# A fused attention and expert kernel: a new order of the first attention batch on all engines

## The chip, the cores and the metric

The kernel runs on one core of one Trainium2 chip. The metric is the device time of one execution in microseconds (us). TensorE is PE in the profile, VectorE DVE, ScalarE ACT, GpSimd POOL and SyncE SP. SP issues nearly all of the DMAs.

## The reference, cut to what matters

x is (2, 512, 1024), the context (2, 1024, 1024). Both x (after a layer norm) and the context are rounded to 8-bit integers, multiplied, and added to x. A second layer norm follows, then a gate that picks two of eight experts per token, and their matmuls.

```python
q1 = fake_quant(layernorm(x), s1, z1); q2 = fake_quant(ctx, s2, z2)   # (clip(round(v / s + z), 0, 255) - z) * s
x = x + tanh(g_xattn) * matmul(q1, q2)
y = layernorm(x)
top = top_k(y @ W_gate + b_gate, 2)
x = x + tanh(g_ffn) * mean over top of relu(y @ W_e + b_e)
```

## The kernel before, in words

Rows are handled in tiles of 128. There are eight x tiles (0 to 3 are batch 0, 4 to 7 batch 1) and sixteen context tiles (0 to 7 are batch 0). Every tile is 128 by 1024. There are three stages: the attention with the second layer norm and the gate (to about 90 us in the profile), the selection of experts (to about 109 us), and 20 expert slots, each 48 matmuls and 8 transposes.

The order of the work is written out by hand, one list for each engine, and every engine works its list strictly in order. Counting semaphores join the lists. All lines below are those of the profile.

A context tile k goes through these steps: SP loads it into one of eight slots of `stage` (`load_ctx`, L298; tile 8+k waits until tile k has been quantised), ACT or DVE writes it as 8-bit integers (`quantise_ctx`, L525 and L790, into one of four buffers `u8c`, so it waits for the centring of tile k-4), and POOL or DVE subtracts 128 and writes bf16 (`centre_ctx`, L424 and L795, tile `q2`). PE then adds its columns up (`column_sum`, L1057) and multiplies x tiles with it (`attend`, L1065).

An x tile i goes through these: SP loads it (`load_x`, L301), DVE takes mean and variance (`x_stats`, L744 and L746), ACT takes the root (`std`, L531), DVE makes scale and shift of two tiles at once with seven small operations (`scales`, L759 to L766), ACT or DVE writes 8-bit integers (`quantise_x`, L569 and L776), POOL or DVE centres them (`centre_q1`, L438 and L784), PE transposes (`transpose_q1`, L1050), ACT copies the result from PSUM (`keep_q1T`, L536), PE multiplies with the eight context tiles of the batch (`attend`), and then adds a correction that needs the batch's column sums (`fold`, L1072). DVE adds the product to x (`x_new`, L808), takes the second layer norm's statistics (`stats(1, ...)`), scales (L759 to L769), and DVE or ACT writes y (`normalise`, L802 and L549). PE transposes y (`transpose_y`, L1097), ACT copies it (`keep_yT`, L556), and PE makes the gate's product (`gate`, L1124: f32 matmuls with 8 columns each).

The column sums of a batch are copied by ACT (`keep_colsum_hi`, L541) when the eighth context tile has been added, and DVE then writes what the bf16 copy lost (`keep_colsum_lo`, L738). `fold` waits for that. `split_d` (L716 to L723) is a chain of small DVE operations that `fold` needs too. In `attend_after(i)` PE waits for an earlier `x_new`, since two PSUM slabs take turns, and for the tile's `keep_q1T`.

The expert weights of expert 0 are loaded into the same `stage` slots (`load_w0`, L305) and split by ACT (`split_hi0`, L561) and DVE (`split_lo`, L880).

Of the kernel before, what the change touches and what calls it, by code (L numbers as in the profile page):

```python
# [5 lines left out]
def flamingo_gated_moe(nc, x, ctx_kv, small, W_gate, W_e, b_e, out):  # L6
# [15 lines left out]
    KT = D // P  # L22
# [11 lines left out]
    NCH = 4  # L34
# [12 lines left out]
    with ctx:  # L47
# [186 lines left out]

        ACT_CTX = (0, 1, 2, 3, 4, 5, 8, 9, 10, 11, 12, 13, 14, 15)
        DVE_CTX = (6, 7)
        POOL_CEN = (0, 1, 2, 3, 5, 7, 8, 9, 10, 11, 12, 13, 14, 15)
        DVE_CEN = (4, 6)
        ACT_X, DVE_X = (0, 1, 2, 4, 5, 6, 7), (3,)
        POOL_Q1, DVE_Q1 = (0, 1, 2, 6), (3, 4, 5, 7)  # L240
        ACT_Y, DVE_Y = (1, 2, 6, 7), (0, 3, 4, 5)

        def wait_quantised_ctx(eng, k):
# [50 lines left out]
        def _(sp):  # L294
            def load_ctx(k):
                if k >= CB:
                    wait_quantised_ctx(sp, k - CB)
                sp.dma_start(stage[:, k % CB, :], ctx_t[k]).then_inc(s_ctx[k % CB], 16)  # L298

            def load_x(i):  # L300
                sp.dma_start(xt[:, i, :], x_t[i]).then_inc(s_x[i], 16)  # L301

            def load_w0(c):
                wait_quantised_ctx(sp, KT + 2 * c + 1)
                sp.dma_start(stage[:, CK * c:CK * (c + 1), :], w_t[:, 0, CK * c:CK * (c + 1), :]).then_inc(s_w[c], 16)  # L305
# [14 lines left out]

            for i in (0, 1):
                load_x(i)
            for k in (0, 1):
                load_ctx(k)
            load_x(2)
            load_ctx(2)
            load_x(3)
            for k in range(3, KT):
                load_ctx(k)
            for j in range(TPB):  # L330
                load_x(TPB + j)
                load_ctx(KT + j)
            sp.dma_start(wg[:, :, :], W_gate.rearrange("(k p) e -> p k e", p=P)).then_inc(s_wg, 16)
            for k in range(KT + TPB, 2 * KT):
                load_ctx(k)
            load_w0(0)
            load_w0(1)
            store_y(0)
            store_y(1)
            load_w0(2)  # L340
            load_w0(3)
            store_x_new(0)
            store_x_new(1)
            store_y(2)
# [46 lines left out]
        def _(pool):  # L391
# [49 lines left out]
            centre_ctx(1)  # L441
            centre_q1(0)
            centre_ctx(2)
            centre_q1(1)
            centre_ctx(3)
            centre_ctx(5)
            centre_ctx(7)
            centre_ctx(8)
            centre_q1(2)
            for k in range(KT + 1, 2 * KT):  # L450
                centre_ctx(k)
            pool.wait_ge(s_att, TPB)
            pool.iota(iota_pe[:, :, :], [[1, P], [0, E]], base=0, channel_multiplier=0,
                      allow_small_or_imprecise_dtypes=True).then_inc(s_iota, 1)
# [6 lines left out]
            add_rowsum(0)  # L461
            add_rowsum(1)
            centre_q1(6)
            add_rowsum(2)
            add_rowsum(3)

# [50 lines left out]
        def _(act):  # L517
            act.dma_start(par[:, :], small.partition_broadcast(P)).then_inc(s_par, 16)

            def quantise_ctx(k):  # L520

                act.wait_ge(s_ctx[k % CB], 16 * (k // CB + 1))
                if k >= 4:
                    wait_centred_ctx(act, k - 4)
                act.activation(u8c[:, k % 4, :], stage[:, k % CB, :], ACT.Identity, scale=dv(INV2),  # L525
                               bias=par[:, 3:4]).then_inc(s_uc, 1)

            def std(which, i, n, count):
# [65 lines left out]
            act.activation(drv[:, TX:TF + 1], par[:, 4:6], ACT.Tanh).then_inc(s_tanh, 1)  # L594
            act.wait_ge(s_const, 1)
            act.activation(lnv[:, 0, T1, 0:1], eps[:, :], ACT.Sqrt)
            std(0, 0, 2, 1)
            quantise_ctx(0)
            quantise_ctx(1)
            quantise_x(0)  # L600
            quantise_ctx(2)
            quantise_x(1)
            std(0, 2, 2, 2)
            quantise_ctx(3)
            keep_q1T(0)
            quantise_ctx(4)
            keep_q1T(1)
            quantise_ctx(5)
            quantise_x(2)
            quantise_ctx(8)  # L610
            keep_q1T(2)
            keep_colsum_hi(0)
            quantise_ctx(9)
            std(0, 4, 2, 3)
            quantise_ctx(10)
            quantise_x(4)
            quantise_ctx(11)
            keep_q1T(3)
            quantise_ctx(12)
            quantise_x(5)  # L620
            quantise_ctx(13)
            std(1, 0, 2, 1)
            quantise_ctx(14)
            normalise(1)
            quantise_ctx(15)
            keep_yT(0)
            keep_q1T(4)
            keep_q1T(5)
            std(1, 2, 2, 2)
            keep_yT(1)  # L630
            keep_colsum_hi(1)
            std(0, 6, 2, 4)
            normalise(2)
            sum_q1(4)
            quantise_x(6)
            quantise_x(7)
            split_hi0(0)
            keep_yT(2)
            keep_q1T(6)
            std(1, 4, 1, 3)  # L640
            sum_q1(5)
            keep_yT(3)
# [53 lines left out]
        def _(dve):  # L696
# [192 lines left out]
            scales(0, 0, 2, 1)  # L889
            x_stats(2)  # L890
            derive()
            x_stats(3)
            scales(0, 2, 2, 2)
            quantise_x(3)
            centre_q1(3)
            centre_ctx(4)
            quantise_ctx(6)
            centre_ctx(6)
            quantise_ctx(7)
            split_d()  # L900
            x_stats(4)
            x_stats(5)
            keep_colsum_lo(0)
            x_new(0)
            scales(0, 4, 2, 3)
            x_new(1)
            stats(1, 0, 0)
            centre_q1(4)
            stats(1, 1, 1)
            x_stats(6)  # L910
            x_new(2)
            scales(1, 0, 2, 1)
            normalise(0)
            x_new(3)
            read_rowsums()
            centre_q1(5)
            stats(1, 2, 0)
            stats(1, 3, 2)
            x_stats(7)
            scales(1, 2, 2, 2)  # L920
            keep_colsum_lo(1)
            scales(0, 6, 2, 4)
            normalise(3)
            x_new(4)
            centre_q1(7)
            stats(1, 4, 3)
            split_lo(0, 1, slice(0, CW))
            x_new(5)
            scales(1, 4, 1, 3)
            normalise(4)  # L930
            stats(1, 5, 4)
# [104 lines left out]
        def _(pe):  # L1036
# [120 lines left out]
                    wait_centred_ctx(pe, k)  # L1157
                    column_sum(k)

            column_sums(0, 2)  # L1160
            transpose_q1(0)
            column_sums(2, 3)
            transpose_q1(1)
            pe.wait_ge(s_qe, 1)
            for k in range(3):
                attend(0, k)
            for k in range(3, KT):
                column_sums(k, k + 1)
                attend(0, k)
                if k == KT - 2:  # L1170
                    transpose_q1(2)
            pe.wait_ge(s_qe, 2)
            attend_half(1, 0)
            attend_half(1, 1)
            pe.wait_ge(s_dr, 1)
            fold(0)
            fold(1)
            transpose_q1(3)
            for i in (2, 3):
                attend_after(i)  # L1180
# [28 lines left out]
            gate(2)  # L1209
            transpose_q1(7)  # L1210
            attend_half(6, 1)
# [86 lines left out]
```

## Time and profile before

| | us |
|---|---|
| median of 3 runs | 359.78 (358.92 to 360.76) |
| the profiled execution | 359.12, its span 357.4 |
| PE busy | 323.5 (91% of the span) |
| DVE busy | 226.3 (63%) |
| ACT busy | 139.9 (39%) |
| POOL busy | 113.0 (32%) |
| mean granted TensorE clock | 0.964 |

The page's busy times are averages over three stages with different limits. The times in the rows further down are microseconds from the start of the span. "Busy" of PE counts matmuls with modelled ends, so two neighbours overlap in the records, and the distance between starts tells the pace.

### The profile page before, as it was taken

The numbers are of one execution on the slowest core, as the hardware profiler recorded it, in microseconds if no ns is written. First come the engines' busy times: TensorE is split into PE (matmuls) and PEld (weight loads), VectorE is DVE, ScalarE is ACT, GpSimd is POOL, SyncE is SP. The second block draws the span as 40 slices with busy tenths as digits, with TensorE's granted clock in tenths as the row PEclk, the third lists the DMA queues.
The fourth block names the chain that finished last, engine by engine and source line by source line (L and its number), as shares of the span: only waits on it lengthen the run. The fifth ranks groups of instructions, "written<-read, shape, count | busy, mean of one in ns | idle before, by whom it ended". The sixth has DMA issues, their size and how long they took to land.

```text
span 357.4 us, 6929 instructions
## 1 busy us (share of the span) xinstructions
PE 323.5 (91%) x1695; PEld 251.0 (70%) x1704; DVE 226.3 (63%) x345; ACT 139.9 (39%) x124; POOL 113.0 (32%) x135
## 2 busy tenths in 40 slices
PE   0598899999599999999999999999999999999960
PEld 0134366589547888888888888888888888888840
DVE  2898999977889653799668326832349334934220
ACT  3774878789103701656172017201154015401100
POOL 3553464000024023415335335123332333233310
PEclk9999999998579999999999999999999999999995
DMA  6999568475327986799989955975439953455233
GB/s 224 413 409 385 220 253 347 166 261 230 159 85 300 410 285 135 192 383 318 417 251 326 358 125 131 395 237 117 88 103 358 330 109 86 100 116 118 29 88 59
DMA packets 23004, 81.46 MB, mean 228 GB/s; under 512 B 3152, under 2 KB 3152, under 8 KB 22992
## 3 DMA queue, kind: packets, MB, share of 16 engines
q1 hardware_dynamic: 16656, 58.76, 42.9%
q0 software_dynamic: 6192, 22.55, 26.6%
q8 instruction: 6, 0.10, 0.1%
q14 instruction: 6, 0.05, 0.0%
q10 hardware_dynamic: 144, 0.01, 0.0%
HBM read 62.43 MB, written 18.87 MB: 228 GB/s over the span
## 4 chain that ended last, share of the span: by engine, by line
PE 80%; DVE 12%; issue 2%; DMA 2%; POOL 1%; ACT 0%; POOLq 0%; DVEq 0%; ACTq 0%
PE ps L1262 61%; PE ps_y L1238 5%; PE ps L1065 4%; DVE st L744 4%; PE ps_q L1124 2%; PE ps_s L1124 2%; PE ps L1042 2%; PE ps_y L1097 2%; DMA par<-in_small_dram 2%; DVE xt L808 1%; PE ps L1150 1%; PE ps L1072 1%; DVE u8c L790 1%; DVE lnv L760 1%; DVE mv L746 1%
## 5 line engine op out<-in xcount | busy, mean ns | idle before, releaser
L1262 PE MATMUL ps<-w_hi,yT_hi 128*128 x320 | 126.5, 395 | 0.5 <-DVE yT_lo L994 0.5
L1262 PE MATMUL ps<-w_hi,yT_lo 128*128 x320 | 124.8, 390 | 0.0
L1262 PE MATMUL ps<-w_lo,yT_hi 128*128 x320 | 124.5, 389 | 0.0
L880 DVE TENSOR_TENSOR w_lo<-stage,w_hi 128x2048 f32 (+1 forms) x32 | 72.0, 2287 | 13.2 <-ACT w_hi L679 11.8
L679 ACT ACTIVATE w_hi<-stage 128x2048 f32 x28 | 52.5, 1912 | 59.1 <-PE ps L1262 47.2
L504 POOL DMA_INDIRECT out_dram<-res,sidx x20 | 32.5, 1627 | 133.7 <-DVE res L1028 121.1
L1025 DVE TENSOR_TENSOR res<-ps,bias 128x512 f32<-128x512 f32 x40 | 27.6, 689 | 65.5 <-issue 34.1
L1262 PEld LDWEIGHTS ps<-w_hi,yT_hi 128*128 128x128 f32 x320 | 60.1, 188 | 12.7 <-issue 0.9
L1262 PEld LDWEIGHTS ps<-w_hi,yT_lo 128*128 128x128 f32 x320 | 60.1, 188 | 12.8
L1262 PEld LDWEIGHTS ps<-w_lo,yT_hi 128*128 128x128 f32 x320 | 60.2, 188 | 11.8
L666 ACT ACTIVATE yT_hi<-ps_y 128x1024 fp32r<-128x1024 f32 x21 | 21.4, 1020 | 114.5 <-PE ps_y L1238 114.5
L994 DVE TENSOR_TENSOR yT_lo<-ps_y,yT_hi 128x1024 fp32r<-128x1024 f32 x21 | 25.7, 1223 | 19.2 <-ACT yT_hi L666 12.3
L1065 PE MATMUL ps<-q,q1T 128*128 128x512 bf16 x123 | 31.2, 396 | 2.4 <-ACT q1T L536 1.8
L473 POOL DMA_INDIRECT y_rows<-y_scratch,gidx x22 | 24.4, 1109 | 17.7 <-POOL gidx L470 17.7
L470 POOL COPY gidx<-idx 128x1 uint32 x22 | 24.2, 1098 | 6.5 <-PE ps_y L1238 5.1
L1065 PEld LDWEIGHTS ps<-q,q1T 128*128 128x128 bf16 x128 | 12.6, 102 | 17.0 <-issue 3.5
L424 POOL TENSOR_SCALAR q<-u8c 128x1024 bf16<-128x1024 uint8 x14 | 15.5, 1108 | 26.8 <-ACT u8c L525 26.1
L1238 PE MATMUL ps_y<-ident_f,y_rows 128*128 128x128 f32 x168 | 21.8, 273 | 0.0
L1028 DVE TENSOR_SCALAR res<-res,weight 128x512 f32<-128x512 f32 x40 | 19.5, 486 | 3.7 <-DVE res L1025 1.4
L1238 PEld LDWEIGHTS ps_y<-ident_f,y_rows 128*128 128x128 f32 x168 | 19.5, 140 | 3.0 <-DMA y_rows<-y_scratch,idx 0.4
L744 DVE BATCH_NORM_STATS2 st<-xt 128x6 f32<-128x512 f32 x32 | 20.5, 683 | 0.4
L1057 PE MATMUL ps_y<-q,ones_b 128*128 128x512 bf16 x15 | 6.8, 542 | 12.9 <-POOL q L424 12.8
(163 smaller groups left out, 264.7 us busy)
## 6 DMA issues: line engine op xcount, KB each, us to landing
stage<-in_L_ffn_W_e_dram SPq DMA_DIRECT2D x32, 1024.0 KB, 7.3
stage<-in_ctx_dram SPq DMA_DIRECT2D x16, 512.0 KB, 11.6
xt<-in_x_dram SPq DMA_DIRECT2D x8, 512.0 KB, 11.4
y_scratch<-y SPq DMA_DIRECT2D x8, 512.0 KB, 3.9
out_dram<-xt SPq DMA_DIRECT2D x8, 512.0 KB, 3.0
bias<-in_L_ffn_b_e_dram SPq DMA_DIRECT2D x8, 512.0 KB, 4.2
y_rows<-y_scratch,gidx POOLq DMA_INDIRECT x22
out_dram<-res,sidx POOLq DMA_INDIRECT x20, 6.4
```

Of the source, the lines that this page charges most:

```text
L470: pool.tensor_copy(gidx[:, q:q + 1], idx[:, bass.ds(col, 1)]).then_inc(s_pool, 1)
L473: pool.indirect_dma_start(out=y_rows[q][:, :], out_offset=None, in_=y_dram[:, :], in_offset=bass.IndirectOffsetOnAxis(ap=gidx[:, q:q + 1], ...
L504: pool.indirect_dma_start(out=out_rows[:, :], out_offset=bass.IndirectOffsetOnAxis(ap=sidx[:, q:q + 1], axis=0), in_=res[q][:, :], in_offs ...
L666: act.activation(yT_hi[q][:, :, :], ps_y[:, :, :], ACT.Copy).then_inc(s_eh, 1)
L679: act.activation(w_hi[:, bass.ds((nxt & 1) * WSZ + c * CW, CW)], stage[:, CK * c:CK * (c + 1), :].rearrange("p k h -> p (k h)"), ACT.Copy) ...
L744: last = dve.bn_stats(st[:, which, h, :], xt[:, i, h * 512:(h + 1) * 512])
L880: dve.tensor_tensor(w_lo[:, dst], stage[:, CK * c:CK * (c + 1), :].rearrange("p k h -> p (k h)"), w_hi[:, dst].bitcast(f32), ALU.subtract) ...
L994: dve.tensor_tensor(yT_lo[q][:, :, :], ps_y[:, :, :], yT_hi[q][:, :, :].bitcast(f32), ALU.subtract).then_inc(s_el, 1)
L1025: dve.tensor_tensor(res[q][:, half], ps[q][:, half], bias[:, bass.ds((woff >> 3) + h * 512, 512)], ALU.add).then_inc(s_free, 1)
L1065: pe.matmul(ps[slab(i)][:, h * 512:(h + 1) * 512], q1T[:, i, k % KT, :], q2[:, k, h * 512:(h + 1) * 512], start=(k % KT == 0), stop=False)
L1238: last = pe.transpose(ps_y[:, k, :], y_rows[q][:, k * P:(k + 1) * P], ident_f[:, :])
L1262: last = pe.matmul(ps[q][:, h * 512:(h + 1) * 512], lhs[q][:, k, :], w[:, bass.ds(woff + k * D + h * 512, 512)], start=(k == 0 and lhs is ...
```

## The change

The lists of all five engines are changed in the attention stage. On SP, context tile 2 is loaded ahead of x tile 2, x tile 3 after context tile 7, and x tiles 6 and 7 after all context tiles. The four loads of expert 0's weights stand together ahead of the first stores of y. Context tiles 6 and 7 are centred on DVE (before: 4 and 6), tile 4 and 5 on POOL. Tiles 4, 5 and 7 of x are centred on POOL and no longer on DVE. ACT quantises context tiles ahead of the roots and x tiles. DVE does the quantising and centring of context tiles 6 and 7 before the statistics of x tile 3, and does the statistics of x tiles 6 and 7 after `keep_colsum_lo(1)`. PE adds up three context tiles first, transposes x tile 2 after the two folds, adds up the second batch's eight context tiles ahead of x tile 5's transpose, and transposes each y tile later in the list. Nothing that is computed changes.

```diff
-        POOL_CEN = (0, 1, 2, 3, 5, 7, 8, 9, 10, 11, 12, 13, 14, 15)
-        DVE_CEN = (4, 6)
+        POOL_CEN = (0, 1, 2, 3, 4, 5, 8, 9, 10, 11, 12, 13, 14, 15)
+        DVE_CEN = (6, 7)
-        POOL_Q1, DVE_Q1 = (0, 1, 2, 6), (3, 4, 5, 7)
+        POOL_Q1, DVE_Q1 = (0, 1, 2, 4, 5, 6, 7), (3,)
...
 # SP
-            for k in (0, 1):
+            for k in (0, 1, 2):
                 load_ctx(k)
             load_x(2)
-            load_ctx(2)
-            load_x(3)
             for k in range(3, KT):
                 load_ctx(k)
+            load_x(3)
+            load_ctx(KT)
+            load_ctx(KT + 1)
+            load_x(4)
+            load_ctx(KT + 2)
+            load_x(5)
...
-            load_w0(0)
-            load_w0(1)
+            load_x(6)
+            load_x(7)
+            for c in range(NCH):
+                load_w0(c)
             store_y(0)
             store_y(1)
-            load_w0(2)
-            load_w0(3)
...
 # ScalarE
+            act.wait_ge(s_inv, 1)
+            quantise_ctx(0)
             std(0, 0, 2, 1)
-            quantise_ctx(0)
             quantise_ctx(1)
+            quantise_ctx(2)
             quantise_x(0)
-            quantise_ctx(2)
             quantise_x(1)
+            quantise_ctx(3)
+            quantise_ctx(4)
+            keep_q1T(0)
+            quantise_ctx(5)
+            keep_q1T(1)
+            quantise_ctx(8)
+            keep_colsum_hi(0)
             std(0, 2, 2, 2)
...
+            quantise_ctx(15)
+            quantise_x(4)
             quantise_x(5)
...
             keep_q1T(4)
             keep_q1T(5)
-            std(1, 2, 2, 2)
+            std(1, 0, 2, 1)
+            keep_colsum_hi(1)
+            normalise(1)
+            keep_yT(0)
+            sum_q1(4)
+            std(0, 6, 2, 4)
             keep_yT(1)
...
             quantise_x(6)
             quantise_x(7)
+            std(1, 2, 2, 2)
             split_hi0(0)
+            keep_q1T(6)
+            normalise(2)
             keep_yT(2)
-            keep_q1T(6)
...
 # VectorE
             derive()
+            split_d()
+            quantise_ctx(6)
+            quantise_ctx(7)
+            centre_ctx(6)
+            centre_ctx(7)
             x_stats(3)
             scales(0, 2, 2, 2)
+            keep_colsum_lo(0)
             quantise_x(3)
             centre_q1(3)
...
+            x_new(0)
             x_stats(4)
+            x_new(1)
             x_stats(5)
+            x_new(2)
             scales(0, 4, 2, 3)
             stats(1, 0, 0)
+            x_new(3)
             stats(1, 1, 1)
+            read_rowsums()
             scales(1, 0, 2, 1)
             normalise(0)
+            keep_colsum_lo(1)
+            x_stats(6)
+            x_stats(7)
             stats(1, 2, 0)
+            scales(0, 6, 2, 4)
+            x_new(4)
             stats(1, 3, 2)
             scales(1, 2, 2, 2)
             normalise(3)
+            x_new(5)
...
 # TensorE
-            column_sums(0, 2)
+            column_sums(0, 3)
             transpose_q1(0)
-            column_sums(2, 3)
             transpose_q1(1)
+            column_sums(3, 4)
...
             fold(0)
             fold(1)
+            transpose_q1(2)
             transpose_q1(3)
...
             column_sums(KT, KT + 4)
             transpose_q1(4)
-            transpose_y(0)
-            column_sums(KT + 4, KT + 6)
+            column_sums(KT + 4, 2 * KT)
             pe.wait_ge(s_rs, 1)
             transpose_q1(5)
-            transpose_y(1)
-            column_sums(KT + 6, 2 * KT)
             attend_after(4)
             attend_half(4, 0)
-            gate(0)
+            transpose_y(0)
             attend_half(4, 1)
             fold(4)
-            transpose_y(2)
+            transpose_y(1)
+            gate(0)
...
             fold(5)
-            transpose_y(3)
+            transpose_y(2)
             attend_after(6)
             attend_half(6, 0)
+            transpose_y(3)
             gate(2)
```

## Rows read from the trace of the kernel before

**Rows 1.** Busy time by stretch: start:end, length, five engines, PEclk, DMA share, GB/s

```profile
34.50:56.50 22.00, 20.37 (x146) 11.51 (x150) 20.82 (x44) 16.69 (x19) 10.30 (x11) 1.00 0.70 269
56.50:90.30 33.80, 33.64 (x237) 26.18 (x240) 27.61 (x66) 29.28 (x33) 3.67 (x3) 0.94 0.63 241
90.30:109.00 18.70, 14.31 (x111) 8.82 (x111) 16.44 (x50) 1.42 (x2) 3.38 (x5) 0.66 0.32 113
```

**Rows 2.** The chain that ended last: start, length, engine, tile, line

```profile
28.37 0.38 PE ps_y L1057
...
33.21 1.30 DVE xt L808
...
55.21 1.23 DVE cs L738
...
70.86 0.54 PE ps L1072 x2
```

**Rows 3.** Timeline of PE: start, length, line, operation, output, shape, count, idle time before

```profile
19.20 2.74 PE L1065 MATMUL ps<-q,q1T 128*128 128x512 bf16 x6 [0.79 <-ACT q1T L536]
...
24.86 0.59 PE L1057 MATMUL ps_y<-q,ones_b 128*128 128x512 bf16 x2
...
34.55 3.63 PE L1065 MATMUL ps<-q,q1T 128*128 128x512 bf16 x16 [0.40 <-DVE xt L808]
...
46.72 1.09 PE L1097 MATMUL ps_y<-ident_f,y 128*128 128x128 f32 x8
...
51.06 1.89 PE L1065 MATMUL ps<-q,q1T 128*128 128x512 bf16 x7
52.78 1.85 PE L1124 MATMUL ps_s<-wg,yT 128*128 128x8 f32 x16
```

**Rows 4.** Timeline of ACT

```profile
29.28 1.02 ACT L541 ACTIVATE cs<-ps_y 128x1024 bf16<-128x1024 f32 x1
30.18 1.24 ACT L525 ACTIVATE u8c<-stage,par,drv 128x1024 uint8<-128x1024 f32 x1
31.31 0.29 ACT L531 ACTIVATE lnv<-mv,eps 128x2 f32<-128x2 f32 x1
...
60.31 1.89 ACT L561 ACTIVATE w_hi<-stage 128x2048 fp32r<-128x2048 f32 x1
```

**Rows 5.** Timeline of DVE

```profile
10.45 0.17 DVE L759 RECIPROCAL lnv<-lnv 128x2 f32<-128x2 f32 x1 [0.43 <-ACT lnv L531]
...
11.30 0.23 DVE L764 TENSOR_SCALAR lnv<-lnv,drv 128x2 f32<-128x2 f32 x1
...
11.76 0.90 DVE L766 TENSOR_SCALAR lnv<-lnv,par 128x2 f32<-128x2 f32 x1
...
22.96 1.53 DVE L790 TENSOR_SCALAR u8c<-stage,drv,par 128x1024 uint8<-128x1024 f32 x1
...
50.24 1.29 DVE L744 BATCH_NORM_STATS2 st<-xt 128x6 f32<-128x512 f32 x2
51.56 0.21 DVE L746 BATCH_NORM_AGGREGATE mv<-st 128x2 f32<-128x12 f32 x1
...
58.03 0.81 DVE L802 TENSOR_SCALAR y<-xt,lnv 128x1024 f32<-128x1024 f32 x1
```

**Rows 6.** Timeline of POOL

```profile
11.57 2.17 POOL L424 TENSOR_SCALAR q<-u8c 128x1024 bf16<-128x1024 uint8 x2 [7.67 <-ACT u8c L525]
...
22.40 1.55 POOL L424 TENSOR_SCALAR q<-u8c 128x1024 bf16<-128x1024 uint8 x1 [3.01 <-ACT u8c L525]
```

**Rows 7.** Timeline of SP: the issues of context tile 0 and of x tile 4

```profile
1.77 0.42 SPq L298 DMA_DIRECT2D stage<-in_ctx_dram  x1
...
7.30 0.46 SPq L301 DMA_DIRECT2D xt<-in_x_dram  x1
```

**Rows 8.** The same two among the DMA issues: count, KB, us from issue to landing

```profile
stage<-in_ctx_dram SPq DMA_DIRECT2D x1, 512.0 KB, 7.3
...
xt<-in_x_dram SPq DMA_DIRECT2D x1, 512.0 KB, 14.6
```

More of the change, by code:

```diff
@@ L322, in _ @@
                 load_x(i)
-            for k in (0, 1):
+            for k in (0, 1, 2):
                 load_ctx(k)
             load_x(2)
-            load_ctx(2)
-            load_x(3)
             for k in range(3, KT):
                 load_ctx(k)
-            for j in range(TPB):
-                load_x(TPB + j)
-                load_ctx(KT + j)
+            load_x(3)
[4 more added lines that the diff above has]
+            load_x(5)
+            load_ctx(KT + 3)
+            load_ctx(KT + 4)
             sp.dma_start(wg[:, :, :], W_gate.rearrange("(k p) e -> p k e", p=P)).then_inc(s_wg, 16)
-            for k in range(KT + TPB, 2 * KT):
+            for k in range(KT + 5, 2 * KT):
                 load_ctx(k)
-            load_w0(0)
-            load_w0(1)
+            load_x(6)
+            load_x(7)
+            for c in range(NCH):
+                load_w0(c)
             store_y(0)
             store_y(1)
-            load_w0(2)
-            load_w0(3)
             store_x_new(0)
@@ L441, in _ @@
             centre_ctx(1)
+            centre_ctx(2)
             centre_q1(0)
-            centre_ctx(2)
             centre_q1(1)
             centre_ctx(3)
+            centre_ctx(4)
             centre_ctx(5)
-            centre_ctx(7)
             centre_ctx(8)
+            centre_ctx(9)
+            centre_ctx(10)
             centre_q1(2)
-            for k in range(KT + 1, 2 * KT):
+            for k in range(KT + 3, 2 * KT):
                 centre_ctx(k)
+            centre_q1(4)
+            centre_q1(5)
             pool.wait_ge(s_att, TPB)
@@ L463, in _ @@
             centre_q1(6)
+            centre_q1(7)
             add_rowsum(2)
@@ L596, in _ @@
             act.activation(lnv[:, 0, T1, 0:1], eps[:, :], ACT.Sqrt)
+            act.wait_ge(s_inv, 1)
+            quantise_ctx(0)
             std(0, 0, 2, 1)
-            quantise_ctx(0)
             quantise_ctx(1)
+            quantise_ctx(2)
             quantise_x(0)
-            quantise_ctx(2)
             quantise_x(1)
-            std(0, 2, 2, 2)
[L604 to L608, printed above, removed]
+            quantise_ctx(3)
[5 more added lines that the diff above has]
+            keep_colsum_hi(0)
+            std(0, 2, 2, 2)
+            quantise_ctx(9)
+            quantise_ctx(10)
             quantise_x(2)
-            quantise_ctx(8)
+            quantise_ctx(11)
             keep_q1T(2)
[L612 to L617, printed above, removed]
             keep_q1T(3)
             quantise_ctx(12)
-            quantise_x(5)
[L621 to L626, printed above, removed]
+            quantise_ctx(13)
+            quantise_ctx(14)
+            std(0, 4, 2, 3)
+            quantise_ctx(15)
+            quantise_x(4)
+            quantise_x(5)
             keep_q1T(4)
             keep_q1T(5)
-            std(1, 2, 2, 2)
+            std(1, 0, 2, 1)
[4 more added lines that the diff above has]
+            std(0, 6, 2, 4)
             keep_yT(1)
[L631 to L634, printed above, removed]
             quantise_x(6)
             quantise_x(7)
+            std(1, 2, 2, 2)
             split_hi0(0)
+            keep_q1T(6)
+            normalise(2)
             keep_yT(2)
-            keep_q1T(6)
             std(1, 4, 1, 3)
@@ L891, in _ @@
             derive()
+            split_d()
[3 more added lines that the diff above has]
+            centre_ctx(7)
             x_stats(3)
             scales(0, 2, 2, 2)
+            keep_colsum_lo(0)
             quantise_x(3)
             centre_q1(3)
[L896 to L900, printed above, removed]
+            x_new(0)
             x_stats(4)
+            x_new(1)
             x_stats(5)
-            keep_colsum_lo(0)
-            x_new(0)
+            x_new(2)
             scales(0, 4, 2, 3)
-            x_new(1)
             stats(1, 0, 0)
-            centre_q1(4)
+            x_new(3)
             stats(1, 1, 1)
-            x_stats(6)
-            x_new(2)
+            read_rowsums()
             scales(1, 0, 2, 1)
             normalise(0)
-            x_new(3)
-            read_rowsums()
-            centre_q1(5)
+            keep_colsum_lo(1)
+            x_stats(6)
+            x_stats(7)
             stats(1, 2, 0)
+            scales(0, 6, 2, 4)
+            x_new(4)
             stats(1, 3, 2)
-            x_stats(7)
             scales(1, 2, 2, 2)
-            keep_colsum_lo(1)
-            scales(0, 6, 2, 4)
             normalise(3)
-            x_new(4)
-            centre_q1(7)
+            x_new(5)
             stats(1, 4, 3)
             split_lo(0, 1, slice(0, CW))
-            x_new(5)
             scales(1, 4, 1, 3)
@@ L1158, in column_sums @@
                     column_sum(k)
-            column_sums(0, 2)
+            column_sums(0, 3)
             transpose_q1(0)
-            column_sums(2, 3)
             transpose_q1(1)
+            column_sums(3, 4)
             pe.wait_ge(s_qe, 1)
-            for k in range(3):
+            for k in range(4):
                 attend(0, k)
-            for k in range(3, KT):
+            for k in range(4, KT):
                 column_sums(k, k + 1)
                 attend(0, k)
-                if k == KT - 2:
-                    transpose_q1(2)
             pe.wait_ge(s_qe, 2)
```

## The prediction

> **What bounds the kernel now.** I read the busy times by stretch first [rows 1]. From 34.50 us to 90.30 PE is the bound: it is busy 20.37 of 22.00 us and then 33.64 of 33.80. From 90.30 to 109.00 it waits on the selection, and behind that the slots follow at a fixed pace. No work outside the attention stage changes, so the question is only how far the end of that stage moves. I then read the chain of waits for where PE depended on others [rows 2]: the last column sum of batch 0 at 28.37, `x_new(0)` at 33.21 (it frees PE for x tile 2), `keep_colsum_lo(1)` at 55.21 (`fold(4)` waits for it), and `fold(6)` at 70.86 + 0.54 = 71.40. From there on both lists have the same PE order, and PE is dense. So I work out when `fold(6)` ends after the change; the difference to 71.40 is the difference of the whole. It splits at the start of `attend(2)`, 34.55 before [rows 3].
>
> **Prices.** PE: an x tile against eight context tiles is 3.6 us with the fold 4.1, half of it 1.72 (51.06 to 52.78), a y transpose 0.93 (the 1.09 without its overlap), a gate 1.71 (1.85 without it) [rows 3]; two matmuls of 512 columns start to start take 0.84 at 19.20 (six in 2.53) and 0.44 from 24.86 on. These are the two levels of the clock, 1.2 and 2.4 GHz, though the granted clock is given as 1.00 for both. ACT: a copy 0.90 (29.28 to 30.18), a quantisation 1.13 in a row and 1.24 to its end, a root 0.29, a weight split 1.89 [rows 4]. DVE: statistics of a tile 1.54 (50.24 to 51.56 + 0.21), seven small operations of a `scales` 1.6 or, in the second norm, five in 1.0 (0.2 each, 10.45 to 11.76), y 0.81, `keep_colsum_lo` 1.23, `x_new` 1.30 [rows 2, 5]. POOL: a centring 1.04 [rows 6]. An idle engine starts about 0.06 after its releaser, DVE 0.4 after a root starts.
>
> **Where DVE and POOL collide.** DVE's L764 takes 0.23, and L766, a like operation, takes 0.90 with POOL's centring (11.57 to 12.61) beside it [rows 5, 6]: it ends at 12.66, when POOL's first one does. The quantisation at 22.96 took 1.53, not 0.81, beside POOL's of 22.40, itself 1.55. So such an operation waits for the other engine's to end. The Trainium skill says so too (SBUF — State Buffer, "Who interferes with whom"): whoever issues first holds the shared pair of ports for the whole instruction, and the other one blocks. This case's trace agrees (0.90 against 0.23). By a reading without that rule the sum below would be 1.4 us less. The rule speaks against this change, which puts POOL's first centrings on top of the first `scales`.
>
> **Part 1: up to the start of attend(2).** Loads: context tile 0 lands at 1.77 + 7.3 = 9.07, x tile 4, ten transfers later, at 21.90, so 1.28 a tile [rows 7, 8]. In the new order context tile 2 lands at 11.6, x tile 2 at 12.9, context tiles 3 to 7 from 14.2 to 19.3 (1.28 earlier each), x tile 3 at 20.6 (6.4 later), context tile 8 at 21.9. x tiles 6 and 7 land by 37; their use is after 50. The bytes are the same.
> - ACT quantises context tile 0 at 9.15 to 10.38 and is then behind with the root: DVE begins `scales` at 10.68 (before 10.45). POOL now centres at 10.46 to 11.5, 11.8 to 12.8 and 13.0 to 14.0. Three operations of `scales` are caught, one by each, so it ends at 14.05 and not at 12.66. x tile 0 is quantised at 14.1 to 15.3, x tile 1 to 16.5, POOL centres them by 16.5 and 17.6, and PE transposes from 16.55. ACT then does two context tiles ahead of `keep_q1T(0)`, which ends at 19.65. `attend(0)` starts at 19.7 (19.20 before). The gain in loading is not in it.
> - DVE ends `split_d` at 20.35 (the same 3.6 with POOL beside it as before, now ahead of the context tiles), quantises tiles 6 and 7 to 22.6 and centres them to 23.95.
> - PE from 19.7: 11 units of 0.86 or 0.44 us (one context tile's sum or product) to the last column sum. Before, the pace rose at 24.3, 5.1 us behind the dense start at 19.20. PE is dense from 16.55 now, so I take 21.7; at once would give the last sum at 24.7, as late as before 26.3. Taken: T = 25.5, where it was 28.75.
> - Behind T: ACT's copy to T + 1.05, the root, `scales` for x tiles 2 and 3 from T + 1.4 (new there; the root stood ahead of this before), its last operation caught by POOL, to T + 3.55, `keep_colsum_lo(0)` to T + 4.8, then the folds. `quantise_x(3)` to T + 5.65, `centre_q1(3)` behind POOL's `centre_q1(2)` to T + 7.1, `x_new(0)` to T + 8.45. `attend(2)` starts at T + 8.5 = 34.0. Before, from 28.75 to 34.55 it took 5.8. So 3.25 us gained at T shrink to 0.55.
>
> **Part 2: from attend(2) at 34.0 to fold(6).** PE's work is the same, 71.40 - 34.55 = 36.85 less 1.6 idle (22.00 - 20.37) = 35.25. I look for PE's new waits.
> - `x_new(1)` is done at 36.8, so `attend(3)` follows at once; with fold to 42.1. Row sums, four context sums, the transpose of x tile 4 (POOL has it at 44.2, after `scales(0, 4)` to 41.8), four sums to 47.0, the transpose of x tile 5 to 47.55, the first half of `attend(4)` to 49.2. No wait so far.
> - `transpose_y(0)` wants y(0). Its root now stands on ACT behind `keep_q1T(5)`, which waits for PE's 47.55: copy 47.6, root 48.5, `scales` to 49.9, y(0) at 50.75. **PE waits 1.6.** Then y transpose 51.75, half 53.45, `fold(4)` 54.0 (`keep_colsum_lo(1)`, 51.95, no longer holds it), y transpose 54.95, gate 56.65, half 58.4, gate 60.1.
> - `transpose_q1(6)`: DVE goes on behind `keep_colsum_lo(1)` with x tiles 6 and 7 and `stats(1, 2)`, 3 x 1.54, to 56.55, `scales(0, 6)` to 58.2, ACT 59.5, POOL 60.6. **PE waits 0.55**, transposes to 61.15, half 62.85, `fold(5)` 63.4.
> - `transpose_y(2)`: `x_new(4)` to 59.5, `stats(1, 3)` to 61.05, root, then on ACT `split_hi0(0)` 61.45 to 63.35, a copy to 64.2, y(2) to 65.4. **PE waits 2.05.** y(3), by DVE at 63.5, is in time, so from 65.45: transpose, half, transpose, gate, q transpose, half, fold: 0.93 + 1.72 + 0.93 + 1.71 + 0.5 + 1.7 + 0.55 = 8.05, `fold(6)` ends at 73.5.
> - Check: 34.0 + 35.25 + 4.2 = 73.45. So +2.1 against 71.40: -0.55 in part 1, +4.2 of new waits, -1.6 of old ones.
>
> **Edits at nothing.** The fourth weight load now stands ahead of the y stores on SP and waits for context tile 15's quantisation, at about 40; y(0) is there at 50.75. Three centrings go from DVE to POOL, which is idle then (10.30 of 22.00 [rows 1]); DVE's relief is what takes `keep_colsum_lo(1)` off the path, and it is in the sum. If the y stores were late, `normalise(4)` would be; it has 7 us to spare.
>
> **The sum.** The profiled execution took 359.12, so 359.12 + 2.1 = 361.2. The median of the runs is 0.66 above it, by which it would be 361.9. I take the middle, 361.5.
>
> **Bounds.** T: -0.8 to +0.8 (pace). Collisions: none caught in the first `scales` takes 0.7 off T (DVE's context tiles then bound), none in the second takes 0.65; one more adds 0.9. The wait for y(0) is 1.3 to 1.9. That for y(2) is at least 0.5, if ACT were free when the scale is ready, at most 2.5. Not all go one way: 0 to +4.3, so 358.9 to 363.9 between the two bases.
>
> **The rivals.**
> - *Faster: the new waits do not appear.* If the roots and y tiles come in time, PE's 35.25 us stand dense behind 33.2 to 34.0: `fold(6)` at 68.5 to 69.3, 2.1 to 2.9 less, 356.2 to 357.3. For it: PE loses nothing through `keep_colsum_lo(1)`, and DVE is relieved. Against: y(0)'s root stands behind a copy that waits for PE, whatever DVE does. Chance 0.14, with halfway cases.
> - *No change: the collisions miss.* They hang on a tenth or two of a microsecond. Without them `attend(2)` starts 0.7 to 1.4 earlier, and the sum is +0.7 to +1.4: 360.2 to 360.8. Chance 0.38, with the case that y(2) is less late.
> - *Slower still: the clock falls in the waits.* From 90.30 to 109.00, with PE busy 14.31 of 18.70, the granted clock is 0.66 [rows 1]. If a wait of 1.6 or 2.05 beside gates of 8 columns did that, some 5 us (19.2 to 24.3) would run at 0.84 for 0.44: +2.4, 363.9. Against: waits of 1.0 us did not do it. Chance 0.06.
> - The forecast has the rest, 0.42.
>
> **How the numbers follow.** A measurement can tell 0.5% from nothing, 1.8 us here, so 361.6 is the edge, and the forecast lies on it. I count the forecast's case as slower (what of it falls below the edge, the no-change case's upper end makes up): slower 0.42 + 0.06 = 0.48, same 0.38, faster 0.14. The range leaves out the dense rival's core and the upper bound of all waits together: 358.0 to 364.0.
>
> **What would show it.** In the profile after: `attend(0)` starts near 19.7, the last column sum of batch 0 near 25.5, `attend(2)` near 34.0. PE's list of waits has new ones on ps_y for y (L1097), 1 to 2 us each, released by `normalise`. `fold(6)` ends near 73.5. I am wrong if `attend(2)` starts below 32, or if PE meets y(0) and y(2) without waiting, or if stretches behind 90 us change in length.

## The result, and the profile after

The changed kernel took 364.64 us (median of 4, 364.27 to 364.97) against 359.57: a ratio of 1.0123, 95% interval 1.0098 to 1.0148 (the quotient of the two medians, 1.0141, lies within it). Ratios compare fast executions alone: one that lies over 1.5% above the fastest of its kernel is left out, as the one of 367.07 in run 5. The change is slower, as forecast, but by 5 us and not by 2, and outside the range. The profiled execution took 364.40 with a span of 362.7, against 359.12 and 357.4: 5.28 us to explain.

The busy times of the same three stretches as [rows 1], with the same columns:

```profile
34.50:56.50 22.00, 19.84 (x126) 9.28 (x126) 16.61 (x35) 14.40 (x15) 11.06 (x12) 0.92 0.62 247
56.50:90.30 33.80, 31.61 (x239) 23.97 (x238) 28.78 (x68) 26.99 (x33) 6.43 (x4) 1.00 0.60 224
90.30:109.00 18.70, 14.94 (x115) 11.55 (x115) 15.20 (x52) 4.35 (x5) 1.37 (x2) 0.54 0.34 129
```

PE is less busy in both of the first two, and the granted clock, 1.00 before, is 0.92 in the first. The timeline of PE answers to [rows 3]:

```profile
19.71 3.15 PE L1071 MATMUL ps<-q,q1T 128*128 128x512 bf16 x8
...
25.29 0.59 PE L1063 MATMUL ps_y<-q,ones_b 128*128 128x512 bf16 x2
...
30.83 1.02 PE L1078 MATMUL ps<-cs,d_rows 64*128 64x512 bf16 x4 [1.06 <-DVE cs L747]
...
33.88 0.62 PE L1056 MATMUL ps_s<-ident_b,q 128*128 128x128 bf16 x8 [1.37 <-DVE q L793]
35.20 5.31 PE L1071 MATMUL ps<-q,q1T 128*128 128x512 bf16 x16 [0.70 <-DVE xt L817]
...
40.98 3.63 PE L1071 MATMUL ps<-q,q1T 128*128 128x512 bf16 x16
...
53.59 1.09 PE L1103 MATMUL ps_y<-ident_f,y 128*128 128x128 f32 x8 [1.46 <-DVE y L811]
...
63.51 0.62 PE L1056 MATMUL ps_q<-ident_b,q 128*128 128x128 bf16 x8 [0.43 <-POOL q L441]
...
68.15 1.09 PE L1103 MATMUL ps_y<-ident_f,y 128*128 128x128 f32 x8 [1.76 <-ACT y L557]
...
75.65 0.60 PE L1078 MATMUL ps<-cs,d_rows 64*128 64x512 bf16 x2
```

The reader is to see four things. `attend(0)` starts at 19.71, and the last column sum starts at 25.29, 3.1 us earlier than before. `attend(2)` starts at 35.20, 0.65 later than before; the gain is gone by then. It takes 5.31 us where `attend(3)`, the same 16 matmuls, takes 3.63. Three waits stand behind it, 3.65 us together. `fold(6)` starts at 75.65 and ends at 76.26 by the chain, 4.86 behind 71.40 [rows 2].

The PE busy time and granted clock around `attend(2)` (stretch, length, PE busy, PEclk, DMA share, GB/s):

```profile
34.00:36.00 2.00, 1.30 (x12) 0.98 1.04 414
36.00:38.00 2.00, 2.00 (x7) 0.50 1.03 410
38.00:40.00 2.00, 2.00 (x8) 0.66 1.04 412
40.00:42.00 2.00, 2.00 (x10) 1.00 1.00 397
```

The clock fell to 0.50, its 1.2 GHz level, near 36, and came back before 40. Ahead of it PE had waited 1.06 + 1.37 + 0.70 = 3.13 of the 5.43 us from 29.77 to 35.20, and done only the four matmuls of two folds and two transposes. Before, it had waited 0.40 there [rows 3].

The waits of the kernel before are less than the 1.6 that its busy time leaves. Two lines of its PE:

```profile
39.74 3.40 PE L1065 MATMUL ps<-q,q1T 128*128 128x512 bf16 x15 [1.02 <-ACT q1T L536]
...
70.80 0.60 PE L1072 MATMUL ps<-cs,d_rows 64*128 64x512 bf16 x2
```

The trace has 15 of the 16 matmuls of `attend(3)`, and 7 of 8 in some halves; each missing record of 0.22 us counts as idle. So I take the distance instead. With the changed kernel's 40.98 - 40.45 = 0.53 for a fold, `attend(3)` could have started at 38.11 + 0.53 = 38.64. From there to `fold(6)` it is 70.80 - 38.64 = 32.16. In the changed kernel it is 75.65 - 40.98 = 34.67, of which 3.65 are waits and 31.02 work. The same work leaves 32.16 - 31.02 = 1.14 of old waits.

| where | us |
|---|---|
| start of attend(2), 35.20 - 34.55 | 0.65 |
| attend(2) at the lower clock, 5.25 - 3.56 to the start of its fold | 1.69 |
| waits behind it, 3.65 - 1.14 | 2.51 |
| rounding between there and fold(6) | 0.01 |
| behind fold(6): the last gates (95.24 - 89.51 for 90.11 - 84.65: 0.27) and the rest | 0.42 |
| sum | 5.28 |

### The profile page after: what moved, and what is told of

Read it like the earlier page. It is cut to its first block, busy times and chain, and to the rows that moved or that the text cites. A ratio compares the mean times of both kernels' runs of the same rounds, so it can differ in the third digit from the quotient of the medians.

```text
span 362.7 us, 6937 instructions
## 1 busy us (share of the span) xinstructions
PE 325.6 (90%) x1703; PEld 251.1 (69%) x1704; DVE 225.5 (62%) x342; ACT 140.9 (39%) x124; POOL 118.1 (33%) x138
## 4 chain that ended last, share of the span: by engine, by line
PE 80%; DVE 8%; DMA 3%; issue 3%; ACT 2%; POOL 1%; SPq 0%; POOLq 0%; DVEq 0%; ACTq 0%
PE ps L1266 60%; PE ps L1071 6%; PE ps_y L1242 5%; PE ps_q L1130 2%; DMA stage<-in_ctx_dram 2%; PE ps_y L1103 2%; PE ps_s L1130 1%; DVE st L753 1%; DMA y_rows<-y_scratch,idx 1%; PE ps L1156 1%; PE ps L1063 1%; PE ps_y L1063 1%; DVE xt L817 1%; DVE cs L747 1%; ACT u8c L533 1%
## 5 line engine op out<-in xcount | busy, mean ns | idle before, releaser
L1000 DVE TENSOR_TENSOR yT_lo<-ps_y,yT_hi 128x1024 fp32r<-128x1024 f32 x21 | 25.7, 1222 | 18.9 <-ACT yT_hi L675 12.2
L1071 PE MATMUL ps<-q,q1T 128*128 128x512 bf16 x128 | 33.0, 407 | 0.7 <-DVE xt L817 0.7
L481 POOL DMA_INDIRECT y_rows<-y_scratch,gidx x22 | 24.4, 1111 | 17.7 <-POOL gidx L478 17.7
L1242 PEld LDWEIGHTS ps_y<-ident_f,y_rows 128*128 128x128 f32 x168 | 19.5, 140 | 3.2 <-DMA y_rows<-y_scratch,idx 0.6
L1034 DVE TENSOR_SCALAR res<-res,weight 128x512 f32<-128x512 f32 x40 | 19.5, 486 | 3.6 <-DVE res L1031 0.6
```

The lines of the kernel that those rows point to most:

```text
L481: pool.indirect_dma_start(out=y_rows[q][:, :], out_offset=None, in_=y_dram[:, :], in_offset=bass.IndirectOffsetOnAxis(ap=gidx[:, q:q + 1], ...
L1000: dve.tensor_tensor(yT_lo[q][:, :, :], ps_y[:, :, :], yT_hi[q][:, :, :].bitcast(f32), ALU.subtract).then_inc(s_el, 1)
L1071: pe.matmul(ps[slab(i)][:, h * 512:(h + 1) * 512], q1T[:, i, k % KT, :], q2[:, k, h * 512:(h + 1) * 512], start=(k % KT == 0), stop=False)
L1242: last = pe.transpose(ps_y[:, k, :], y_rows[q][:, k * P:(k + 1) * P], ident_f[:, :])
```

## The experiments

Each ratio is against the kernel before, run beside it on the same chip. The kernels start from the changed one, unless it is said.

**1. Fillers ahead of attend(2).**

```diff
+            fill(4, ps_s[:, :])          # fill: n matmuls of 512 columns into an unused PSUM bank
             fold(0)
             fold(1)
             transpose_q1(2)
+            fill(5, ps_k[:, 0:512])
             transpose_q1(3)
+            fill(3, ps_k[:, 0:512])
```

> The changed kernel with 12 filler matmuls of 512 columns (into PSUM that nobody needs then) in the three gaps of PE ahead of attend(2): 4 before the folds, 5 and 3 behind the transposes of x tiles 2 and 3. Theory (clock): attend(2) took 5.31 us because PE had idled 3.1 us of the 5.4 before it and the granted clock fell to 0.50 behind that. Then it takes 3.6 again, starts no later than 35.3, and the whole is 1.7 us less than the changed kernel: about 362.9. Rival (something else slowed the matmuls, as the DMAs and GpSimd beside them): attend(2) keeps 5.3 and the time stays at 364.6.

Measured: 364.04 (362.57 to 365.82), ratio 1.0099 (1.0072 to 1.0125); the profiled execution took 362.78. Its PE (the line numbers are five higher here):

```profile
34.52 3.63 PE L1076 MATMUL ps<-q,q1T 128*128 128x512 bf16 x15
...
61.17 0.62 PE L1061 MATMUL ps_q<-ident_b,q 128*128 128x128 bf16 x8 [0.43 <-POOL q L441]
61.84 3.00 PE L1076 MATMUL ps<-q,q1T 128*128 128x512 bf16 x7
...
65.81 1.09 PE L1108 MATMUL ps_y<-ident_f,y 128*128 128x128 f32 x8
```

`attend(2)` takes 3.63 with DMAs and POOL beside it as in the changed kernel, so the mechanism is shown. The other traces bear it out. From the start of `attend(2)` to its fold it is 5.25 to 5.77 us in all five kernels with this order and no fillers (the changed one, both of run 4, those of runs 6 and 7), and 3.55 or 3.56 in the three with fillers there (runs 1 to 3).

But the clock now fell at 61.84 (half a tile in 3.00 and not 1.89 us), behind a gate and a short wait. That fall cost nothing by `fold(6)`: the wait of 1.76 for y(2) is gone at 65.81, since PE came later and y(2) was ready. From `attend(2)` to `fold(6)` it is 38.79 us against 40.45, and the profiled execution is 1.6 less than the changed kernel's, both near the 1.7 expected. The median gained little, and the ten times spread over 3 us where the changed kernel's four lay within 0.7. Their mean granted clocks go from 0.949 (at 365.82) to 0.963 (at 363.11).

**2. Fillers in every gap.** Six more ahead of `transpose_y(0)`, two ahead of `transpose_q1(6)`, seven ahead of `transpose_y(2)`.

> The changed kernel with filler matmuls of 512 columns in every gap of PE: the 12 ahead of attend(2), and 6 ahead of transpose_y(0), 2 ahead of transpose_q1(6), 7 ahead of transpose_y(2). Theory (new waits, and a clock that falls because of them, at one place or another from execution to execution): the granted clock stays at 1.00 up to the last gates, attend(2) takes 3.6 us, and what is left against the kernel before are the waits alone, 3.65 us less the 1.6 of old ones: fold(6) ends near 73.2, 2 us behind the kernel before (ratio 1.005 to 1.006), with less spread than the 12 fillers alone. Rival (the fillers delay PE, or the clock is not what they touch): ratio 1.010, as with the 12 alone.

Measured: median 364.56, ratio 1.009 (1.0053 to 1.0127). The nine times lie in two groups: 361.07, 361.09 and 361.50, and six from 364.30 to 365.68. By the medians (364.56 and 360.03) the quotient would be 1.0126. The profile is of the lower group (361.50):

```profile
19.60 2.31 PE L1076 MATMUL ps<-q,q1T 128*128 128x512 bf16 x8
...
24.34 0.59 PE L1068 MATMUL ps_y<-q,ones_b 128*128 128x512 bf16 x2
...
34.25 3.63 PE L1076 MATMUL ps<-q,q1T 128*128 128x512 bf16 x16
...
73.05 0.60 PE L1083 MATMUL ps<-cs,d_rows 64*128 64x512 bf16 x2
```

and its granted clock by stretch:

```profile
28.00:44.00 16.00, 15.43 (x108) 1.00 1.04 397
44.00:84.00 40.00, 39.69 (x276) 1.00 0.54 202
```

With the clock at 1.00 throughout, `fold(6)` starts at 73.05 and ends near 73.6, 2.2 behind the kernel before. That is the forecast's sum (73.5), but in part by luck. The last column sum starts at 24.34, 0.95 ahead of the changed kernel's 25.29, since PE's pace rose sooner in `attend(0)` (2.31 for its eight matmuls, there 3.15). The fillers stand behind that, so they are not the reason. From the last column sum to `attend(2)` it is 9.91 in both. With the changed kernel's own start, 35.20, the same 38.80 us would put `fold(6)` at 74.00, 3.2 behind the kernel before.

The median did not follow. The mean granted clock is on record for each execution: 0.964 or 0.965 in the lower group, 0.958 or 0.959 in the upper. So a fall of the clock goes with the 3 us between them, in spite of the fillers. Where it falls then is not known, as no trace of the upper group was kept.

**3. Fillers behind the gates too.** Three more behind each of gates 0 to 4, where PE has no gap.

> As the kernel with fillers in every gap, and 3 more fillers of 512 columns behind each of gates 0 to 4, where PE has no gap: 15 x 0.22 = 3.2 us of added work, about 3.0 on PE's path. Theory (the gates' 8-column matmuls are what lets the clock fall, and the executions of the kernel with filled gaps near 364.5 are those in which it fell behind a gate): no execution falls there, the times lie in one group, at 361.3 + 3.0 = 364.3, as low as the slow group before it although PE does 3 us more. Rival (the slow group has another cause, a DMA or GpSimd): two groups again, 364.3 and 367.6.

Measured: 366.24, six times within 0.9 us (366.14 to 367.04), ratio 1.0154 (1.0124 to 1.0185).

```profile
28.00:84.00 56.00, 54.89 (x372) 1.00 0.67 250
84.00:97.00 13.00, 13.00 (x80) 0.70 0.62 251
```

One group, as the theory had it, and the clock holds to 84. But it lies 1.9 above what was expected. Nine of the 15 fillers stand ahead of `fold(6)`, 1.9 us, so run 2's 73.05 would become 75.0; it starts at 74.73, and the stretch up to there is not the reason. The last gates run from 90.23 to 96.91, 6.68 us, against 5.46 before and 5.31 in run 2, and the transpose ahead of them is slow as well: the clock falls earlier against them. Why there is only one group is thus not wholly shown. The fillers may also just have moved the falls to the end.

**4. The waits for y(0) and y(2).** On ScalarE, alone and then both:

```diff
             keep_q1T(4)
+            std(1, 0, 2, 1)
             keep_q1T(5)
-            std(1, 0, 2, 1)
...
-            split_hi0(0)
             keep_q1T(6)
             normalise(2)
+            split_hi0(0)
```

> The changed kernel with the root for y tiles 0 and 1 (std(1, 0)) ahead of keep_q1T(5) on ScalarE, not behind it. Theory (the chain over DVE binds): the 1.46 us that PE waits for y(0) go, but x tile 6 and y(2) come only as much earlier as DVE starts keep_colsum_lo(1) earlier, 1.1 us, and PE's waits there grow by 0.3: 1.1 us less, 363.5. Rival (PE's waits add up): 1.46 less, 363.2, with the later waits as they were (0.43 and 1.76). Second rival (it moves on): nothing, the wait reappears at transpose_y(2), 364.6.

> As the run before (root for y(0) first), and also split_hi0(0) behind normalise(2) on ScalarE instead of ahead of keep_q1T(6). Theory: y(2) then comes 1.2 us behind its scale and PE's wait for it falls from 1.76 to about 0.4; together 2.5 us less than the changed kernel, 362.1. Rival (DVE's chain to the scale of y(2) is what binds, ScalarE's order is cover): no more than the run before, 363.5.

Measured: 364.53, ratio 1.0118 (1.0069 to 1.0167), and 365.33, ratio 1.0116 (1.0061 to 1.0170). No gain that can be told. PE in the first:

```profile
52.71 1.04 PE L1103 MATMUL ps_y<-ident_f,y 128*128 128x128 f32 x8
...
63.10 0.62 PE L1056 MATMUL ps_q<-ident_b,q 128*128 128x128 bf16 x8 [0.96 <-POOL q L441]
63.77 3.14 PE L1071 MATMUL ps<-q,q1T 128*128 128x512 bf16 x7
...
67.74 1.09 PE L1103 MATMUL ps_y<-ident_f,y 128*128 128x128 f32 x8
...
75.24 0.60 PE L1078 MATMUL ps<-cs,d_rows 64*128 64x512 bf16 x2
```

The wait for y(0) is gone, and that for x tile 6 has grown from 0.43 to 0.96. From the start of `attend(3)` to that of `fold(6)` it is 75.24 - 41.73 = 33.51, against 34.67 in the changed kernel: 1.16 less, as expected. It is that although the clock fell at 63.77 (granted 0.61 from 63.0 to 66.8) and took about 1.2: PE comes to y(2) so much later, at 67.74, that the wait of 1.76 is gone, and the fall costs nothing by `fold(6)`. What hid the gain lies outside. `attend(3)` started 0.75 later (41.73 for 40.98), 0.23 of it ahead of the last column sum and 0.52 in `attend(2)`, where the clock fell earlier; and PE waited 0.51 for a y tile's copy behind `fold(6)`.

In the second kernel `fold(6)` starts at 73.63, 2.0 earlier than in the changed one, 0.7 of it from an earlier last column sum. But the clock fell again, where no wait stood behind to take it up:

```profile
82.76 3.19 PE L1071 MATMUL ps<-q,q1T 128*128 128x512 bf16 x7 [0.20 <-issue]
```

The last gates took 6.69 us there for 5.73, and ended 2.4 later than the changed kernel's.

**5. x_new(0) first on VectorE.**

```diff
+            x_new(0)
             quantise_x(3)
             centre_q1(3)
-            x_new(0)
...
 # TensorE, in the loop over x tiles 2 and 3 (and no longer ahead of it)
                 attend_half(i, 0)
+                if i == 2:
+                    transpose_q1(3)
                 attend_half(i, 1)
```

> The changed kernel with x_new(0) ahead of quantise_x(3) and centre_q1(3) on DVE, and PE transposing x tile 3 between the two halves of attend(2) instead of ahead of it. Theory (the collisions of DVE with GpSimd and the queue behind the folds set the start of attend(2)): it starts at 33.6, when keep_q1T(2) is done, instead of 35.2; PE idles 2.2 instead of 3.1 us before it, so the clock may hold: 1.6 us less if it falls all the same (363.0), 3.2 less if it holds (361.4). Rival (x tile 3, now 1.3 us later, becomes the wait at attend(3)): no gain, 364.6.

Measured: 364.20 (361.46 to 367.07), ratio 1.0077 (1.0044 to 1.0109). `attend(2)` starts at 33.59, as expected, 8.42 behind the last column sum and not 9.91. The clock holds over it (1.00) without a filler, behind waits of 1.06 and 1.21, 2.27 us together for 3.13. In the profiled execution, 365.41, it fell later (stretch, length, PE busy, PEclk, DMA share, GB/s):

```profile
62.00:66.00 4.00, 3.95 (x17) 0.64 0.00 0
66.00:71.00 5.00, 4.59 (x19) 0.61 0.75 301
```

**6. GpSimd waits for VectorE.** One line, `pool.wait_ge(s_q1, 1)`, ahead of `centre_ctx(11)`.

> The changed kernel with GpSimd waiting for centre_q1(3) of VectorE before it centres context tile 11. Theory (collision): centre_q1(3) takes 0.7 instead of 1.41 us, x_new(0) and attend(2) start 0.7 earlier (34.5 for 35.2); the clock falls all the same; 0.3 to 1.0 less than the changed kernel, within what 3 rounds can tell. Rival (the length of that operation is its own): 1.41 as before.

Measured: 363.78, ratio 1.0089 (1.0053 to 1.0126). The operations on VectorE in the changed kernel, and then in this one (its line numbers are one higher):

```profile
28.34 0.16 DVE L774 SCALAR_TENSOR_TENSOR lnv<-mv,lnv 128x2 f32<-128x2 f32 x1
28.53 0.90 DVE L775 TENSOR_SCALAR lnv<-lnv,par 128x2 f32<-128x2 f32 x1
29.47 1.22 DVE L747 TENSOR_TENSOR cs<-ps_y,cs 32x1024 bf16<-32x1024 f32 x1
30.72 1.67 DVE L785 TENSOR_SCALAR u8x<-xt,lnv 128x1024 uint8<-128x1024 f32 x1
32.42 1.41 DVE L793 TENSOR_SCALAR q<-u8x 128x1024 bf16<-128x1024 uint8 x1
```

```profile
28.36 1.04 DVE L775 SCALAR_TENSOR_TENSOR lnv<-mv,lnv 128x2 f32<-128x2 f32 x1
29.44 1.11 DVE L776 TENSOR_SCALAR lnv<-lnv,par 128x2 f32<-128x2 f32 x1
...
31.84 1.66 DVE L786 TENSOR_SCALAR u8x<-xt,lnv 128x1024 uint8<-128x1024 f32 x1
33.53 0.69 DVE L794 TENSOR_SCALAR q<-u8x 128x1024 bf16<-128x1024 uint8 x1
```

The centring takes 0.69 and not 1.41: the collision is shown. But `attend(2)` started at 35.60, where 34.5 was expected: the same execution lost more elsewhere. POOL's centring began at 28.35, 0.01 ahead of the small operation at 28.36, which then took 1.04 and not 0.16. In the changed kernel POOL began at 28.34 too, and the operation slipped through. Nothing in the lists decides that. The 1.67 of `quantise_x(3)` stays (1.66): the edit does not touch the centring beside it.

**7. The load order of before, all else changed.**

> The changed kernel with the load order of the kernel before for the first batch (x tile 2 ahead of context tile 2, x tile 3 ahead of context tile 3), all other lists as changed. Theory (the earlier landing of the context tiles is not on the path: PE's first products wait for the quantised x tiles, and context tile 7 waits for VectorE): no change against the changed kernel, 364.6, attend(0) within 0.1 of 19.7. Rival (the loads do bound batch 0): 1.3 us more, 365.9.

Measured: 364.90, ratio 1.0115 (1.0074 to 1.0157), against 1.0123 for the changed kernel. The interval alone would hardly exclude the rival's 1.3 us; the trace does: `attend(0)` starts at 19.60 (19.71 in the changed kernel) and the last column sum at 25.00 (25.29). The earlier loads bring nothing.

**8. The repairs together.** As expected below; the second time without the swap on VectorE.

> The changed kernel with what the runs so far point to, together: root for y(0) ahead of keep_q1T(5), split_hi0(0) behind normalise(2), x_new(0) ahead of quantise_x(3), x tile 3 transposed between the halves of attend(2), scales(0, 4) ahead of x_new(2), and fillers ahead of the folds (4), of attend(2) (5) and of transpose_q1(6) (4). Theory (order behind the folds loses what the earlier context tiles gain): attend(2) starts near 33.3, no wait above 1 us behind it, fold(6) ends at 70.5 to 71.5 against 71.4 before: ratio 0.997 to 1.001. Rival (DVE's chain has no slack, each repair moves the wait): ratio 1.007 as with x_new first alone.

> The repaired kernel without its swap on VectorE, that is with x_new(2) ahead of scales(0, 4) as in the changed kernel. Theory (the swap made the waits of 1.5 us for x_new(2) and 0.7 us for the row sums): both go, a wait of 0.85 for q1 of x tile 4 comes; 1.3 us less than the repaired kernel, fold(6) at 71.9 to 72.0 where the clock holds, ratio 1.003 to 1.005. Rival: the ratio stays at 1.0085, as the clock's falls make up the most of it.

Measured: 363.94, ratio 1.0085 (1.0056 to 1.0114), and 361.81 (360.71 to 364.34), ratio 1.0037 (1.0011 to 1.0063). The swap was a mistake: it made PE wait 1.5 us for `x_new(2)` and 0.7 for the row sums. Without it PE waits 0.85, 0.30 and two gaps that fillers cover, and `fold(6)` starts at 71.17, 0.4 behind the kernel before (from `attend(2)` on 1.33 less than with the swap, as expected):

```profile
71.17 0.60 PE L1083 MATMUL ps<-cs,d_rows 64*128 64x512 bf16 x2
...
79.78 3.18 PE L1076 MATMUL ps<-q,q1T 128*128 128x512 bf16 x7 [0.22 <-issue]
```

In that execution (363.97) the clock fell at 79.78, in `attend(7)`. It is the changed order at its best here, and not better than the old one.

**9. One part alone, and from the kernel before.** GpSimd centres x tiles 4, 5 and 7 in the kernel before; then also:

```diff
             quantise_ctx(10)
+            keep_q1T(3)
             quantise_x(4)
             quantise_ctx(11)
-            keep_q1T(3)
```

> The kernel before with one part of the change alone: GpSimd centres x tiles 4, 5 and 7 instead of VectorE, each at its old place among the context tiles. Theory: VectorE is relieved of 3.4 us (1.16, 0.68 and 1.55), but PE is dense from 34.5 on and waited for it only 0.1 us at fold(4) and 1.0 at attend(3): 0 to 0.8 us less, ratio 0.998 to 1.000. Rival (GpSimd's extra operations hit VectorE's small ones): up to 0.8 more.

> The kernel before with GpSimd centring x tiles 4, 5 and 7, and keep_q1T(3) ahead of quantise_x(4) on ScalarE, which is idle there for 3.4 us, instead of behind quantise_ctx(11). Theory (from attend(2) on PE is the bound in that kernel, and its one wait of 1 us there is for this copy): the wait of 1.02 ahead of attend(3) goes and fold(6) ends 1 us earlier, near 70.4: ratio 0.996 to 0.998. Rival (the time reappears at fold(4) or in the clock): ratio 0.9995 to 1.002.

Measured: 360.17 beside 360.03, ratio 0.9995 (0.9969 to 1.0020), and 360.00 beside 360.65, ratio 0.9973 (0.9952 to 0.9995). The second is the only kernel here whose interval lies below 1, and that by 0.0005 only; among so many kernels it might be chance, but its trace shows the gain. Its PE:

```profile
34.59 3.63 PE L1067 MATMUL ps<-q,q1T 128*128 128x512 bf16 x16 [0.40 <-DVE xt L813]
...
38.91 3.40 PE L1067 MATMUL ps<-q,q1T 128*128 128x512 bf16 x15 [0.16 <-issue]
...
69.72 0.60 PE L1074 MATMUL ps<-cs,d_rows 64*128 64x512 bf16 x2
```

The wait of 1.02 ahead of `attend(3)` is down to 0.16, and `fold(6)` starts at 69.72 and not 70.80: 1.1 us. (Both waits have a missing record of 0.22 in them.)

## Why the prediction was wrong

- **Part 1, up to the last column sum: right.** `attend(0)` at 19.7 was 19.71. T, taken as 25.5, was 25.29 + 0.4 = 25.7. The three collisions in the first `scales` were there, and it ended at 14.1 (14.05 worked out). That loading is not on the path is shown by run 7. The upper bound of T was worked out too low: with the pace rising 5.1 behind 19.7, as before, the 11 units end at 27.0 and not at 26.3. In the traces of runs 1 to 8 the eight matmuls of `attend(0)` take from 2.02 to 3.50 us, and T goes from 24.4 to 25.95, so one trace says little on this term.
- **Part 1, from T to attend(2): 1.0 us too little.** 8.5 was worked out, 9.5 measured. I let VectorE's `quantise_x(3)` win against POOL. It lost, 1.67 and not 0.81; the 1.41 of `centre_q1(3)` was in the sum. The Trainium skill (SBUF — State Buffer, "Who interferes with whom") lets issue order decide. Run 6 agrees for the small operation, where 0.01 us did. For `quantise_x(3)` the records do not show it: VectorE's starts at 30.72 and GpSimd's centring at 30.79, and it is VectorE's that takes twice its time. The upper bound of "one more collision, 0.9" held this. With T it makes the start 35.20, not 34.0.
- **Part 2, "PE's work is the same", 35.25 us: the step that failed.** The lists have the same work, but it ran at two clocks. `attend(2)` was priced at 3.6, and took 5.25 to its fold, 1.7 more, because of the 3.13 us idle ahead of it. I had those gaps in my own numbers (folds at T + 4.8, the wait for `x_new(0)`) and never added them up. I looked at waits only as lost time, and put the fall of the clock as a rival with 0.06, at the waits for y, where in this kernel it did not occur. Its price, 2.4, was of the right order (1.7). Run 1 shows the cause: 12 fillers, and 3.63 us. The 35.25 was also 0.46 too low on its own, since 1.6 of old idle time was taken off and only 1.14 was there.
- **Part 2, the new waits: right.** 1.6, 0.55 and 2.05 were forecast, 1.46, 0.43 and 1.76 measured, each with the releaser named. Run 4 shows the y(0) chain as it was told, with its onward growth at x tile 6.
- **The sum.** Run 2's executions at the full clock take 361.07 to 361.50, where the forecast was 361.2 by the profiled base and 361.5 on record. That they meet is in part luck, since in the one that was traced T was 0.95 earlier than in the changed kernel. The changed kernel's own trace gives 5.28 - 1.69 = 3.6 without the fall of the clock, where 2.1 was summed. The missing 3.2 are the clock in `attend(2)` (1.7), the later start (1.2), the old waits (0.46) and what lies behind `fold(6)` (0.42), less 0.55 for new waits shorter than forecast.
- **The range** was too narrow above, since each term's upper end was priced alone. A fall of the clock belonged among the bounds, as did its coming together with one more collision. Either alone would have stayed inside 364.0.
- **Still open:** why the clock fell in some executions of a kernel and not in others, and what each such fall is worth. It is not the change's alone: of the 26 executions of the kernel before beside run 2, 25 lie from 359.11 to 362.65, those up to 360.51 at a mean clock of 0.962 to 0.966 and those above at 0.954 to 0.962. The traces show falls behind gaps and gates, not what decides them.

The Trainium skill (TensorE: Matmul & The Clock Gate, "HAM oscillation — how this bites in real kernels") describes a waiting array that falls to half its rate, so that the next burst starts slow. This case's trace agrees with that, 0.50 from 36 to 38. That section tells of one long wait between bursts; here three waits of 1.06, 1.37 and 0.70 us with short work between them did it.

## What to carry to other kernels

Where PE is the bound, add up its idle time ahead of each dense stretch, not only the waits on the chain: here 3.13 us of gaps cost 1.7 us more in the matmuls behind them. What a fall of the clock costs in the end depends on what follows: where a wait for another engine stood behind it, the wait took it up (runs 1 and 4). An earlier start of a stage is worth what reaches the next stage's first matmul; 3.1 us gained at the last column sum were 0.65 lost at `attend(2)`, because the root, the scale and the centring were queued behind it. When a time is read from few executions, look at which clock each ran at, and when the pace first rose, before a repair is judged: two repairs that gave 1.2 and 1.3 us between `attend(3)` and `fold(6)` did not show in the median.

## What the runs showed of the hardware that had not been expected

- The granted clock can fall in the midst of a stretch in which PE is called 96% busy (3.65 of 3.80): 0.61 from 63.0 to 66.8 us in run 4's first kernel, behind two gates of 8 columns and a wait of 0.96. Even in the fastest kernel (run 9) it was 0.57 from 72 to 76, with PE busy 4.00 of 4.00:

```profile
70.00:72.00 2.00, 2.00 (x18) 1.00 0.50 199
72.00:76.00 4.00, 4.00 (x17) 0.57 0.99 236
```

- One program's executions can lie in two groups 3 us apart that differ in the mean granted clock: 361.07 to 361.50 at 0.964 or 0.965, and 364.30 to 365.68 at 0.958 or 0.959, in run 2.
- The pace of the first dense stretch can rise at different times though the granted clock is given as 1.00: `attend(0)`, eight matmuls from 19.5 to 19.7 us on, took from 2.02 us (the first kernel of run 8) to 3.50 (the first of run 4), and all that follows moved with it.
- A small VectorE operation of two elements per partition takes 0.16 or 1.04 us, as POOL's centring starts at the same time or 0.01 us ahead of it (run 6).
